# Ring loads ahead of the store, early turns and biases through PSUM in a cross-attention and mixture FFN kernel

## The reference

```python
x = x + xattn(layernorm(x), ctx)       # x (16, 112, 256), ctx (16, 375, 256), 16 heads of 16
x = x + ffn(layernorm(x))              # the FFN sees 112 "batches" (tokens) of 16 positions
...
def ffn(h):                            # E = 8 experts, DFF = 1024, C = 256
    x = transpose(h, (1, 0, 2))        # (112, 16, 256)
    r = relu(x @ gW1.T + gb1)
    g = (r @ gW2.T + gb2).mean(axis=1)          # (112, 8): one gate row per token
    W1 = einsum('be,eoi->boi', g, eW1); b1 = g @ eb1
    W2 = einsum('be,eoi->boi', g, eW2); b2 = g @ eb2
    y = relu(einsum('bsi,boi->bso', x, W1) + b1)
    return transpose(einsum('bsi,boi->bso', y, W2) + b2, (1, 0, 2))
```

## Time and profile before

| | |
|---|---|
| median of 3 runs | 881.05 us (874.02 to 884.4) |
| profiled execution | 882.56 us, its span 880.7 us |
| busy: PE, PEld | 727.5 us (83%), 586.7 us (67%) |
| busy: DVE, ACT, POOL | 544.2 us (62%), 497.3 us (56%), 405.7 us (46%) |
| mean granted TensorE clock | 0.929 of 2.4 GHz |
| DMA | 145.98 MB, mean 166 GB/s, queue 60.5% of 16 engines |

### The profile page before, as it was taken

How to read it: one execution, slowest core, us unless ns; L and a number is a source line. 1 busy time by engine, 2 the same in 40 slices (tenths; PEclk the granted TensorE clock), 3 DMA queues, 4 the chain that set the end, 5 groups by cost and what they waited for, 6 DMA issues and landing times.

```text
span 880.7 us, 35744 instructions
## 1 busy us (share of the span) xinstructions
PE 727.5 (83%) x15107; PEld 586.7 (67%) x15107; DVE 544.2 (62%) x803; ACT 497.3 (56%) x781; POOL 405.7 (46%) x510
## 2 busy tenths in 40 slices
PE   2787999999998884679988888898889889888891
PEld 2665777777876653457766666676667667677671
DVE  6766767676678531346666666675567666566671
ACT  3454677676775642255565656565566566656550
POOL 7452455454555164243555445535527355364220
PEclk9799999999999996589999999999899899999997
DMA  7358767666657118566767557675665765675534
GB/s 204 79 152 208 202 159 179 157 176 172 160 157 176 27 54 173 120 180 175 207 187 213 169 165 206 180 207 169 205 182 167 216 180 168 208 204 170 155 79 81
DMA packets 127911, 145.98 MB, mean 166 GB/s; under 512 B 84906, under 2 KB 105498, under 8 KB 121506
## 3 DMA queue, kind: packets, MB, share of 16 engines
q1 hardware_dynamic: 127778, 144.02, 60.5%
HBM read 102.78 MB, written 41.03 MB: 163 GB/s over the span
## 4 chain that ended last, share of the span: by engine, by line
PE 44%; DMA 18%; SPq 14%; POOL 8%; DVE 7%; issue 5%; ACT 2%; ACTq 0%; POOLq 0%; DVEq 0%
PE banks L1754 19%; PE banks L1729 10%; SPq L675 9%; DMA k_stack<-k_dram 8%; DMA ring<-split_dram 6%; PE banks L314 5%; SPq L529 3%; PE banks L1468 2%; PE banks L1427 2%; PE banks L1450 2%; POOL w_rest L834 2%; POOL w_split L838 2%; DMA y<-xmid_dram 1%; DVE wb L1307 1%; SPq L536 1%
## 5 line engine op out<-in xcount | busy, mean ns | idle before, releaser
L1087 ACT ACTIVATE wb<-banks 128x896 f32<-128x896 f32 x281 | 255.1, 918 | 208.8 <-PE banks L1729 208.4
L1307 DVE COPY wb<-banks 128x896 f32<-128x896 f32 x231 | 251.5, 1089 | 177.3 <-PE banks L1729 177.2
L1729 PE MATMUL banks<-spread,ring 64*128 64x112 bf16 x4096 | 156.7, 219 | 54.1 <-DMA ring<-split_dram 51.9
L1729 PEld LDWEIGHTS banks<-spread,ring 64*128 64x128 bf16 x4096 | 113.7, 99 | 109.0 <-issue 101.9
L832 POOL CAST w_split<-w_rest 128x1024 bf16<-128x1024 f32 x32 | 33.2, 1036 | 237.5 <-ACT w_rest L967 220.8
L1177 DVE TENSOR_REDUCE maxima<-banks 112x2 f32<-112x750 f32 x128 | 117.7, 934 | 30.7 <-PE banks L1427 27.7
L1754 PE MATMUL banks<-wb,xt 128*32 128x128 f32 x3584 | 124.9, 281 | 11.3 <-DVE ht L1336 6.8
L1754 PE MATMUL banks<-wb,ht 128*32 128x128 f32 x3584 | 128.9, 286 | 3.5 <-issue 2.9
L893 ACT ACTIVATE probs<-banks 128x448 f32<-128x448 f32 x192 | 100.5, 544 | 26.3 <-PE banks L1450 24.2
L1754 PEld LDWEIGHTS banks<-wb,xt 128*32 128x32 f32 x3584 | 94.4, 112 | 24.7 <-DVE ht L1336 9.5
L1754 PEld LDWEIGHTS banks<-wb,ht 128*32 128x32 f32 x3584 | 97.1, 114 | 16.0 <-issue 5.7
(11 more groups left out here) (131 smaller groups left out, 967.9 us busy)
## 6 DMA issues: line engine op xcount, KB each, us to landing
ring<-split_dram SPq DMA_DIRECT2D x384, 128.0 KB, 3.0
split_dram<-w_split SPq DMA_DIRECT2D x32, 768.0 KB, 4.3
k_dram<-k_parts SPq DMA_DIRECT2D x16, 576.0 KB, 3.6
k_stack<-k_dram SPq DMA_DIRECT2D x32, 288.0 KB
w_nat<-in_w SPq DMA_DIRECT2D x32, 256.0 KB, 4.1
w_nat<-in_w SPq DMA_DIRECT2D x64, 128.0 KB, 3.1
k_stack<-k_dram SPq DMA_DIRECT2D x32, 192.0 KB
c_raw<-in_ctx_t SPq DMA_DIRECT2D x16, 375.0 KB, 5.2
```

The source lines that it names most:

```text
L1087: act.activation(outputs_of(n, q), formed(bank), ACT.Copy).then_inc(form_act, 1)
L1307: dve.tensor_copy(outputs_of(n, q), formed(bank))\
L1729: last = pe.matmul(banks[:, form_bank(half) + t, NQ * r:NQ * r + NQ], ring[rows, 4 * q + r, :], spread[rows], start=True, stop=True)
```

## The change

- In the loop of SyncE load_ring(n + 2, 0) comes first, then load_natural(n + 4), store_split(n + 3) and load_ring(n + 2, 1).
- Chunks 0, 1 and 2 are turned in steps 13, 14 and 15 of the front, through bank 7; their natural loads, splits and stores and the first ring loads move into these steps too. Before, chunks 0 and 1 were turned in the last steps and chunk 2 in the opening.
- The biases are no product of their own. eb (8 x 1280) is cut into three bf16 parts on GpSimd in step 12 and laid over 64 partitions of eb_ring (zeroed first) by six DMAs in step 13. The gate in `spread` is widened to spread_wide. hidden(i, u) starts each bank with four bf16 matmuls of eb_ring and spread_wide and adds z; the values of the first "out" chunks (i = 0) start with four such matmuls.
- z is transposed by four f32 matmuls with the identity over column groups of 32, in place of one transpose, since it adds to what is in PSUM. VectorE takes the ReLU from PSUM; GpSimd's ReLU goes.
- The opening is only the 16 forms of chunk 0. The y loads come after the ring loads of chunk 1 and the store of chunk 2; VectorE waits for them at the first "out" values. The memset of the ring moves from step 12 to 14.

```diff
-        TURN_AHEAD, TURN_EARLY = 3, 2
+        TURN_AHEAD = TURN_EARLY = 3
+        TURN_STEP = B - TURN_EARLY
+        PRODUCT_PARTS = (0, 0, 0, 1, 1, 2)
...
-            return 4 + w if m < TURN_EARLY else 6 + turn_unit(m, w) % 2
+            return 7 if m < TURN_EARLY else 6 + turn_unit(m, w) % 2
...
-                if s.i is None and s.c == LOOP_STEP + 2 * LOOPS:
+                if s.i is None and s.c == TURN_STEP - 1:
+                    sp.wait_ge(q_mm, 2 * NG)
+                    sp.dma_start(eb_rest[:], eb).then_inc(eb_loaded, 16)
                     load_natural(0)
+                if s.i is None and s.c == TURN_STEP:
+                    sp.wait_ge(eb_cut, 4)
+                    sp.wait_ge(eb_zeroed, 1)
+                    for n, piece in enumerate(PRODUCT_PARTS):
+                        sp.dma_start(eb_ring[n:TILE:SLOTS], eb_parts[:, piece]).then_inc(eb_ready, 16)
+                if s.i is None and s.c == TURN_STEP + 1:
+                    load_natural(1)
+                    store_split(0)
+                if s.i is None and s.c == TURN_STEP + 2:
+                    load_natural(2)
+                    load_ring(0, 0)
+                    load_ring(0, 1)
+                    store_split(1)
+                if s.i is None and s.c == TURN_STEP + 3:
+                    load_natural(3)
...
             steps(sp, step)
 
-            load_natural(1)
-            store_split(0)
-            load_ring(0, 0)
-            load_ring(0, 1)
-            load_natural(2)
+            load_ring(1, 0)
+            load_ring(1, 1)
+            store_split(2)
             for slot in range(2):
                 sp.wait_ge(xmid_stored[slot], 16 * B // 2)
...
-            store_split(1)
-            load_ring(1, 0)
-            load_natural(3)
-            load_ring(1, 1)
-            store_split(2)
...
             for n in range(CHUNKS):
+                load_ring(n + 2, 0)
                 load_natural(n + TURN_AHEAD + 1)
                 store_split(n + TURN_AHEAD)
-                load_ring(n + 2, 0)
                 load_ring(n + 2, 1)
...
-                if s.i is None and s.c == LOOP_STEP + 2 * LOOPS:
-                    queries_stored(pool, 3)
-                    pool.wait_ge(q_mm, 2 * NG)
+                if s.i is None and s.c == TURN_STEP - 1:
+                    for g in range(NG):
+                        queries_stored(pool, g)
+                    pool.wait_ge(stack_set, 16)
+                    pool.memset(eb_ring[:], 0.0).then_inc(eb_zeroed, 1)
+                    pool.wait_ge(eb_loaded, 16)
+                    pool.tensor_copy(eb_parts[:, 0], eb_rest[:]).then_inc(eb_cut, 1)
+                    pool.wait_ge(eb_cut, 1)
+                    pool.tensor_tensor(eb_rest[:], eb_rest[:], eb_parts[:, 0], ALU.subtract).then_inc(eb_cut, 1)
+                    pool.wait_ge(eb_cut, 2)
+                    pool.tensor_copy(eb_parts[:, 1], eb_rest[:]).then_inc(eb_cut, 1)
+                    pool.wait_ge(eb_cut, 3)
+                    pool.tensor_tensor(eb_parts[:, 2], eb_rest[:], eb_parts[:, 1], ALU.subtract).then_inc(eb_cut, 1)
+                if s.i is None and s.c == TURN_STEP:
+                    split(0)
+                if s.i is None and s.c == TURN_STEP + 1:
+                    pool.wait_ge(eb_ready, 16 * PRODUCTS)
                     pool.memset(ring[:].rearrange("p s i -> p (s i)").bitcast(F32), 0.0).then_inc(ring_zeroed, 1)
+                    split(1)
...
-                if hidden_before(n):
-                    i = ORDER[n - 1][1]
-                    for u in range(UNITS):
-                        unit_taken(pool, hidden_unit(i, u))
-                        part = ht[:, 4 * UNIT_FROM[u]:4 * UNIT_FROM[u + 1], 0:3:2, :]
-                        pool.tensor_scalar(part, part, 0.0, None, ALU.max).then_inc(relu_done, 1)
...
                 key_copy(new, 0)
+                if s.i is None and s.c >= TURN_STEP:
+                    turned(s.c - TURN_STEP, 0)
                 exp(s, 9)
...
-                dve.tensor_tensor(ht[:, pairs, 0:3:2, :], ps, bias, ALU.add).then_inc(unit_dve, 1)
...
+                dve.tensor_scalar(ht[:, 4 * g.start:4 * g.stop, 0:3:2, :], ps, 0.0, None, ALU.max).then_inc(unit_dve, 1)
...
-            opening(taken_by_dve, lambda k: None, add_b2, lambda m, w: None)
+            for q in range(HALVES):
+                taken_by_dve(0, q)
...
+                    if w == 0:
+                        pe.wait_ge(xmid_done, TURN_STEP + m)
+                    else:
+                        pe.wait_ge(turn_copied, 2 * m + 1)
...
                 key_project(new, 0)
+                if s.i is None and s.c >= TURN_STEP:
+                    turn(s.c - TURN_STEP, 0)
                 scores(s, 9)
...
+                biased = ORDER[n][0] == "out" and ORDER[n][1] == 0
+                if biased:
+                    for j in range(4):
+                        pe.matmul(banks[32 * j:32 * j + 32, 6 + v % 2, P * m:P * m + P],
+                                  spread_wide[:, g, j].rearrange("p h s -> p (h s)"),
+                                  eb_ring[:, DFF + P * ORDER[n][2]:DFF + P * ORDER[n][2] + P], start=True, stop=False)
...
                 for m, g in enumerate(range(g.start, g.stop)):
-                    last = pe.transpose(banks[:, 6 + v % 2, P * m:P * m + P], z[:, g, :], ident[:])
+                    for c in range(0, P, 32):
+                        pe.matmul(banks[c:c + 32, 6 + v % 2, P * m:P * m + P], eb_ring[:, P * i + c:P * i + c + 32],
+                                  spread_wide[:, g].rearrange("p j h s -> p (j h s)"), start=True, stop=False)
+                    for c in range(0, P, 32):
+                        last = pe.matmul(banks[c:c + 32, 6 + v % 2, P * m:P * m + P], z[:, g, c:c + 32], ident[:],
+                                         start=False, stop=True)
...
-            opening(form, bias1, bias2, turn)
+            for q in range(HALVES):
+                form(0, q)
```

More of the change, by code:

```diff
@@ L168, in build @@
         spread = lasting.take("spread", [P, NQ], BF16)
-        b1_t = lasting.take("b1_t", [P, OT, NQ], F32)
+        spread_wide = lasting.take("spread_wide", [P, GRP, 4, 2, B], BF16)
+        eb_ring = lasting.take("eb_ring", [P, DFF + C], BF16)
         xt = lasting.take("xt", [P, IT, PAIRS, 3, B], F32)
@@ L225, in build @@
         h_sums = gate.take("h_sums", [P, 2, NG, NQ], F32)
-        eb_sb = gate.take("eb_sb", [E, DFF + C], F32)
+        biases = Region(start, start + size([P, P // 2, P], BF16))
+        eb_rest = biases.take("eb_rest", [E, DFF + C], F32)
+        eb_parts = biases.take("eb_parts", [E, 3, DFF + C], BF16)
         q_parts = [nc.alloc_sbuf_tensor_at("q_parts0", [P, 3, GB, 2, NQ], BF16, offset=at_probs), q_parts1, q_parts2,
@@ L360, in unit_of @@
             return max(u for u in range(UNITS) if UNIT_FROM[u] <= g)
[L362 to L381, removed]
         def period(n, form, turn, hidden, value):
@@ L1112, in first_values @@
                         .then_inc(unit_act, 1)
-            opening(taken_by_act, bias1, lambda k: None, turned)
+            for q in range(HALVES):
+                taken_by_act(0, q)
             for n in range(CHUNKS):
@@ L1318, in add_value @@
                 kind, i, a = ORDER[n]
+                if (kind, i, a, u) == ("out", 0, 0, 0):
+                    dve.wait_ge(y_loaded, 16 * 8)
                 dst = z[:, g, :] if kind == "in" else y[:, g, P * a:P * a + P]
@@ L1606, in last_steps @@
                     gate_hidden(5)
-                    turn(1, 0)
-                    turn(1, 1)
             def step(s):
@@ L1621, in step @@
                     max_scores(nxt, 0)
+                if s.i is None and s.c > TURN_STEP:
+                    pe.wait_ge(turn_copied, 2 * (s.c - TURN_STEP))
                 value_project(nxt, 0)
@@ L1656, in step @@
                 key_project(new, 1)
+                if s.i is None and s.c >= TURN_STEP:
+                    turn(s.c - TURN_STEP, 1)
             query_transpose(0)
@@ L1742, in value @@
                         half_taken(HALVES * n + HALVES - 3)
-                    if hidden_before(n) and ORDER[n][0] == "out":
-                        pe.wait_ge(relu_done, UNITS * ORDER[n][1] + u + 1)
-                    elif u == 0 and ORDER[n][0] == "out":
-                        pe.wait_ge(relu_done, UNITS * (ORDER[n][1] + 1))
-                m = g - UNIT_FROM[u]
+                    kind, i, a = ORDER[n]
+                    if hidden_before(n) and kind == "out":
+                        unit_taken(pe, hidden_unit(i, u))
+                    elif u == 0 and kind == "out":
+                        unit_taken(pe, hidden_unit(i, UNITS - 1))
+                    if kind == "out" and i == 0:
+                        pe.wait_ge(pads_set, 2)
+                m = g - UNIT_FROM[u]
+                biased = ORDER[n][0] == "out" and ORDER[n][1] == 0
[4 more added lines that the diff above has]
```

(3 more changed lines are left out.)

90 lines of the change are left out of this document (17 added, 73 removed).

## The result

The changed kernel takes 936.95 us (median of 4 executions, 931.89 to 942.49) where the kernel before took 878.47 beside it: a ratio of 1.066, 95% interval 1.057 to 1.076. It is slower by 58 us; the forecast was 15 us, and its range ended at 914.

The account below looks back on a forecast made before the run. TensorE was taken as busiest, slowed by ring loads, store waits and the clock. From period 2 at 394.2, 412 us of periods plus 22 for the clock reach 828.2; with the tail, 896 us, 1.7% slower, range 860 to 914.

Parts of the forecast that it names:

- The rival of the clock that holds: Steady periods: waits of 2.5 to 3.0 us come at the turns without halving the clock; 874 us, chance 0.22.
- As meant: Steady periods: no wait for w_nat, since loads land in time; 818 us in all, chance 0.06.
- Ring half 0 ahead of the load and the store: SyncE's loop: ring wait goes, w_nat comes late; 19 of 26 periods at least 14.7 or 15.2 us.
- the hidden periods: Periods with hidden units: groups cost 0.38 us for 0.14, period 17.8 us (16.0 to 19.5), no load wait behind.
- my 22 us for the clock: Steady periods: 13 of the 19 turns after a new wait are followed by the half clock, adding 22 us.
- I price both at nothing: Front: VectorE and GpSimd excluding each other, by the moved memset (3.1 us) and bias casts (up to 2.7), costs nothing.
- the front as a whole: Front up to spread: delays sum to +10.3 to 10.5 us, spread written at 343.2, not 332.47; bounds 3 and 16.
- Term (a): Front: the bias split on GpSimd ahead of batch 15's key split delays the keys and step 14 by 5.3 us.
- my 4.1: Front, step 14: load_natural(1) lands at 306.4 while TensorE reaches its turn at 302.3; +4.1 us.
- 0.9 for the eb_ring loads: Front: six eb_ring loads take 3.7 us of the queue ahead of the last keys; slack takes most, leaving +0.9.
- The opening: Chunk 0's forms and the y loads: period 1 starts at 377, 13 us before; period 2 at 394.2, 16.3 before.
- The sum: Whole kernel: 412 us from period 2, plus 22 for the clock, tail -2.4; span 894.5, time 896 us.

Follow-up runs that it names:

- e2: Kernel before with only SyncE's loop order changed to ring half 0, natural load, store, ring half 1: 920.46 us, 1.046.
- e3: Kernel before with SyncE's loop order natural load, ring half 0, store, ring half 1: 836.75 us, 0.950.
- e8: e3 with the eight y loads ahead of store 0, ring 0 and natural load 2: 838.14 us, 0.946 of the kernel before.
- e11: Kernel before with natural loads from chunk 4 on issued by GpSimd ahead of the split, SyncE's loop ring half 0, store, ring half 1: 904.39 us, 1.022.
- e12: e11 with ScalarE in place of GpSimd issuing the natural loads, behind its copy of the turn: 884.63 us, 1.001 of the kernel before.
- e9: Changed kernel with the natural load first in SyncE's loop, and split(2) moved behind the two copies that widen spread: 871.8 us in its one execution.
- e10: Changed kernel with natural loads from chunk 4 on issued by GpSimd, SyncE's loop ring half 0, store, ring half 1: 905.57 us, 1.023 of the kernel before.
- e7: Changed kernel, natural load first, hidden-unit groups as two 128-column matmuls, y loads ahead of ring 1 loads and store 2: 843.96 us, 0.954 of the kernel before.

## Why the prediction was right in kind and wrong in size

**Right.** The sign, the place and the chain. The ring wait went, the turn waits for w_nat, the alternation of long and short periods is gone, the store is no longer what holds SyncE, and the order alone moves both bodies by 40 to 45 us. The rival of the clock that holds fell: a double form of 0.93 us follows the wait in 20 of 26 periods, and the granted clock there (0.50 of 2.4 GHz at 656.05 to 656.85) is the lower level, 1.2 GHz; over the 26 periods the mean is 0.91, before 0.95. "As meant" fell too.

**Wrong, the step "Ring half 0 ahead of the load and the store": the size of its loop.** From half formed to the next turn I had 9.1 us for "out" and 8.6 for "in" chunks, 8.9 on average over the 19 periods without hidden units. They measured 9.9 (9.1 to 11.7). Two terms make the difference. Six ring issues took 3.63 to 5.54 us, median 4.05, and the natural load began 4.3 after the half was formed where I had 3.7. From there to the turn it was 5.75 us for four natural loads and 5.3 for two, where I had 5.4 and 4.9. The 3.63 came from one row of the opening, which I called unhindered; of the 17 periods of the kernel before in which the six can be read alone, none was that short (3.68 to 5.47, median 4.7), and in the changed kernel itself only six of the 26 were. The rows that I had not grouped would have told me. This is 0.9 x 19, some 17.5 us. The other side of the loop, from turn to half formed, was 7.6 with the half clock in it, for 7.3: 5 us. Together the 19 periods took 331.6 us, +22 on my 309.

**Wrong, the hidden periods: +12.** I took 17.8 for their work and no wait behind. The groups were cheaper than priced (0.27 for 0.38 us; of my bounds for the bf16 matmuls nearly the zero was true), but these periods begin at half clock too, after a wait (my 22 us for the clock are counted with the 19 periods above): their work took 17.7 to 19.7, 18.3 on average (+3.4 in all), and five of the seven had a wait for w_nat behind them, 8.5 us in all, since their own half is formed at 8.5 to 9.8 us.

**Wrong, the step "I price both at nothing", and the front as a whole; its +4.1 (347.35 for 343.2) is small by luck.** Up to the key split of batch 14 this execution ran 2.8 us ahead of the one of the kernel before. Counted from that split (the start of its k_rest), spread came 95.7 us later, in the earlier trace rows's execution 78.1: +17.6 for my +10.7. In the other traces the body before takes 79.9 to 81.3 (e2, e3, e8, e11, e12) and the changed one 92.0 to 97.4, some 14 more on average. Term (a) holds: from the key split of batch 14 to that of 15 it is 23.4 us in place of 17.7, +5.7 for +5.3. VectorE waited 7.18 for key_rest(15) and TensorE 6.18 for o_norm behind that. The turn of step 14 waited 2.21 for my 4.1. Part of the rest is what I "priced at nothing", VectorE held while GpSimd works:

```profile
307.27 3.51 POOL L824 MEMSET ring<- 128x4096 f32 x1
...
309.32 2.47 DVE L1169 CAST max_parts<-maxima 112x8 bf16<-112x8 f32 x1
...
310.73 1.03 POOL L831 CAST w_split<-w_rest 128x1024 bf16<-128x1024 f32 x1
```

The cast, 0.17 us otherwise, ended at 311.79, behind the memset and also behind split(1)'s first cast (311.76), and TensorE waited 1.69 for it; x_norm then took 2.22 beside split(1)'s subtraction, where I had counted on slack in that step. Beside split(2) the cast of the gate took 2.11 and cost 1.9, and this one e9 shows. Together they are 3.6 us. TensorE also waited 2.53 for k_stack at 297.7, where I had left 0.9 for the eb_ring loads; what made that wait no run tests, and the remainder stays open. The Trainium skill (SBUF — State Buffer, SBUF: two separate sides) says that the loser of such a pair blocks for the whole instruction of the other; the cast's end at 345.90 with the subtraction's at 345.83 agrees. I had cited that page and then let slack absorb it, without looking for VectorE work on the path beside split(2).

**The opening, +6.0 more by period 2** (404.34 for 394.2): 0.9 of it up to period 0, 4.5 up to period 1, 0.6 behind it. The loads behind y landed 13.6 to 14.1 us after issue, as the y block's 15 us had let me expect, but the y loads themselves went out at 362.39, not 355.7, behind store 2 at 361.70; the four natural issues took 7.11 us there.

**The sum.** Front and opening +10.1, steady part +34.1, tail +1.9: 894.5 + 46.1 = 940.6, the measured span but for rounding. So three quarters of this miss is the steady part: one loop, priced with its fastest leg and held to 19 of its 26 periods. Against the median, 936.95, the forecast of 896 misses by 41; the profiled execution is the longest of the four.

## What to carry to other kernels

Where a queue's order is changed, close the loop: an issue that waits for work of this period, and that gates work of the next, gives a period that no other engine can shorten. Price each leg with the median of its rows, not with the cleanest one, and test the loop against every period, those with more work too. A load whose data is free early goes ahead of an issue that must wait: here that place alone separates 0.95 from 1.05.

## What was unexpected

- Moving the natural load off SyncE's queue took its wait away and went with longer landings of its neighbour (ring loads up to 7.6 to 8.8 us, against 4.5 to 5.1 with the load in SyncE's queue), so a second queue brought 885 and 904 us where the right order in one queue gave 837.
- Four bf16 column-group matmuls hid almost wholly under the f32 ones that follow: a group of twelve takes 0.27 us where the f32 ones alone are 0.25.
- A VectorE cast of 8 x 112 elements, 0.20 us by itself, took 2.11 us beside a GpSimd subtraction; one of 112 x 8, 0.17 us by itself, took 2.47 and outlasted two GpSimd instructions in a row, the second of which began after it. In e9 and e10 the same cast took 3.17 and 2.72, again to the end of the second, in e7 1.98, to the end of the first.
- The form with fewer, slower matmuls gave the shorter hidden periods (17.5 against 18.5 us); why is open.
